# Waits and loads moved in four stages of a twelve-stage Perceiver kernel

## What is computed

```python
# layer 0 feed-forward ("fp4"): blocks of 16 are scaled, rounded to the FP4 grid, scaled back
xq, wq = fp4_quant_dequant(x), fp4_quant_dequant(w)
h = silu(xq_linear(x, w_gate)) * xq_linear(x, w_up); y = xq_linear(h, w_down)
# layer 1 cross-attention ("xattn1"): 16 heads of 16, biases bq, bk, bv, bo
attn = softmax(clip(q @ k.T * scale, -1e4, 1e4)); y = (attn @ v) @ Wo + bo
# layer 2 cross-attention ("xattn2"): 16 heads of 64, bias b_o
sim = softmax(q @ k.T * scale); y = (sim @ v) @ w_o + b_o
# layer 3 cross-attention ("xattn3"): one head of 256, both inputs layer-normed with gains and offsets
x1, x2 = layernorm(modality1, ln1_g, ln1_b), layernorm(modality2, ln2_g, ln2_b)
y = softmax((x1 @ Wq + bq) @ (x2 @ Wk + bk).T * E ** -0.5) @ (x2 @ Wv + bv) @ Wo + bo
```

## Time and profile before

| | us |
|---|---|
| median of three runs | 1784.45 |
| the three runs | 1783.11, 1784.45, 1786.04 |
| the profiled execution | 1781.79 |
| its span, first to last instruction | 1779.9 |
| TensorE busy | 1592.1 (89% of the span) |
| VectorE busy | 1069.7 (60%) |
| ScalarE busy | 849.0 (48%) |
| GpSimd busy | 771.7 (43%) |

### The profile page before, as it was taken

How to read it: one execution, slowest core, us unless ns; L and a number is a source line. 1 busy time by engine, 2 the same in 40 slices (tenths; PEclk the granted TensorE clock), 3 DMA queues, 4 the chain that set the end, 5 groups by cost and what they waited for, 6 DMA issues and landing times. The chain is left out here.

```text
span 1779.9 us, 37424 instructions
## 1 busy us (share of the span) xinstructions
PE 1592.1 (89%) x13583; PEld 1347.5 (76%) x13583; DVE 1069.7 (60%) x3001; ACT 849.0 (48%) x2446; POOL 771.7 (43%) x924
## 2 busy tenths in 40 slices
PE   7999999888886999987799999989978968859998
PEld 6898998756556999955799988965658934549997
DVE  5888887446855888845676677647971132363332
ACT  5666666355335888842566666641003312213332
POOL 7656656243338999833211111116743411212332
PEclk9999999999998999999999999999988987989999
DMA  8555454110023334302433333325028265771222
GB/s 274 168 174 161 151 174 153 64 63 2 1 83 98 137 130 139 119 19 71 171 122 102 125 104 103 126 79 182 1 54 263 29 179 163 249 243 35 37 38 30
DMA packets 127221, 205.30 MB, mean 115 GB/s; under 512 B 21034, under 2 KB 92362, under 8 KB 126530
## 3 DMA queue, kind: packets, MB, share of 16 engines
q1 hardware_dynamic: 119746, 193.61, 33.4%
q0 software_dynamic: 6720, 8.79, 3.2%
q10 hardware_dynamic: 576, 0.52, 0.1%
HBM read 162.54 MB, written 41.14 MB: 114 GB/s over the span
## 5 line engine op out<-in xcount | busy, mean ns | idle before, releaser
L879 DVE TENSOR_SCALAR xattn_oT<-banks,xattn_last 128x256 f32<-128x256 f32 x256 | 111.7, 478 | 90.8 <-PE banks L699 90.6
L785 ACT ACTIVATE xattn_probs<-banks,xattn_negmax 128x257 f32<-128x257 f32 x256 | 123.6, 483 | 67.5 <-DVE xattn_negmax L860 67.5
L1110 POOL TENSOR_SCALAR xattn_probs<-xattn_probs,xattn_rsum 128x257 f32<-128x257 f32 x128 | 119.6, 935 | 30.0 <-DVE xattn_rsum L1351 29.8
L790 ACT ACTIVATE xattn_probs<-xattn_probs,xattn_rsum 128x257 f32<-128x257 f32 x256 | 131.8, 515 | 1.4 <-DVE xattn_rsum L864 1.4
L860 DVE TENSOR_REDUCE xattn_negmax<-banks 128x1 f32<-128x257 f32 x256 | 106.4, 415 | 34.7 <-PE banks L672 33.3
L679 PE MATMUL banks<-ident,xattn_probs 128*128 128x128 f32 x512 | 104.2, 286 | 8.5 <-ACT xattn_probs L790 8.0
L796 ACT CAST xattn_probsT_hi<-banks 128x256 fp32r<-128x256 f32 x256 | 95.4, 372 | 32.7 <-PE banks L679 28.6
L869 DVE TENSOR_TENSOR xattn_probsT_lo<-banks,xattn_probsT_hi 128x256 fp32r<-128x256 f32 x256 | 104.9, 410 | 9.8 <-ACT xattn_probsT_hi L796 8.7
L617 POOL COPY ctx_stat<-xattn_mv 128x2 f32<-128x2 f32 x32 | 6.0, 187 | 238.2 <-DVE xattn_mv L893 238.2
L668 PE MATMUL banks<-xattn_ctxT,xattn_qk_hi 128*128 128x258 f32 x256 | 93.9, 367 | 0.5 <-POOL xattn_ctxN L585 0.3
L573 POOL TENSOR_SCALAR xattn_ctxT<-xattn_rawT 128x514 fp32r<-128x514 f32 x32 | 49.8, 1558 | 98.7 <-issue 94.4
(11 more groups left out here) (500 smaller groups left out, 5250.8 us busy)
## 6 DMA issues: line engine op xcount, KB each, us to landing
xattn_ctxT<-ctx_partsT SPq DMA_DIRECT2D x64, 516.0 KB, 4.0
xattn_ctxN<-ctx_partsN SPq DMA_DIRECT2D x64, 384.0 KB, 4.1
ctx_partsT<-xattn_ctxT SPq DMA_DIRECT2D x32, 516.0 KB, 2.8
moe_w<-in_L_ffn_W SPq DMA_DIRECT2D x16, 1024.0 KB, 13.6
ctx_partsN<-xattn_ctxN SPq DMA_DIRECT2D x32, 384.0 KB, 3.8
moecap_w_early<-in_L_ffn_w SPq DMA_DIRECT2D x10, 1024.0 KB, 9.2
xattn_N<-in_ctx_tiles SPq DMA_DIRECT2D x8, 776.0 KB
xattn_rawN<-in_ctx SPq DMA_DIRECT2D x32, 192.0 KB, 2.8
```

The source lines that it names most:

```text
L785: nc.scalar.activation(probs[:, n % RING, :], SB[n % 2][:, 0:KV], ACT.Exp, bias=negmax[:, n % RING:n % RING + 1], accum_out=psum[:, n % RI ...
L790: nc.scalar.mul(probs[:, n % RING, :], probs[:, n % RING, :], rsum[:, n % RING:n % RING + 1]).then_inc(norm_ready, 1)
L879: nc.vector.tensor_scalar(oT[k][:, heads, b, :], by_head(OB[:, k * 2 * P:(k + 1) * 2 * P]), last[:, k, j * PER_TILE + b:j * PER_TILE + b + ...
L1110: nc.gpsimd.tensor_scalar(probs[:, n % RING, :], probs[:, n % RING, :], rsum[:, n % RING:n % RING + 1], None, ALU.mult).then_inc(norm_read ...
```

## The change

Four edits, one in each stage.

1. xattn1: ScalarE's wait for wv and bv is moved from t = 0 into `values`.
2. xattn2: SP issues `raw_last` and raw rows 0 behind the parts of batch 0, and raw rows 1 behind the parts of batch 1. Raw rows 2 and 3 stay where they were.
3. fp4: ScalarE copies the turned chunk 0 out behind `x_parts(1)` and not behind `x_parts(3)`.
4. xattn3: `rstd` and `last_stat` become part of `ShortWeights` and are loaded at the end of SP's program for scan (22 DMAs on its semaphore and not 17). SP issues keys and rows of tiles 0 to 2 and keys 3, and then only keys 4 to 7. Rows 3 to 7 are issued by ScalarE, each behind `normalise(t - 3)`.

```diff
--- before.py
+++ after.py
@@ -357,6 +357,7 @@
     VALUES = (6, 7, 8, 9)
     PROJECT = {11: range(0, 3), 13: range(3, 6), 15: range(6, 8)}
     M_FILLS, M_START = 1 + GROUPS, 3
+    EARLY_ROWS = 2
     with ExitStack() as ctx:
         st = Stage(core, ctx, name)
         ln = Norm(st, shared=True, first=first)
@@ -476,6 +477,12 @@
                 sp.dma_start(ctxT[:, b].bitcast(F32), core.partsT[n]).then_inc(T_loaded[b], 16)
                 sp.dma_start(ctxN[:, b].bitcast(F32), core.partsN[n]).then_inc(N_loaded[b], 16)
 
+            def load_rows(n):
+                b = n % PER_TILE
+                if n >= PER_TILE:
+                    sp.wait_ge(stats_done, (n - PER_TILE + 1) * KCH)
+                sp.dma_start(raw[:, b], d["ctx_768"][n, 0:KCH * P, :].rearrange("(c p) f -> p c f", p=P)).then_inc(raw_loaded[b], 16)
+
             def keep_parts(n):
                 b = n % PER_TILE
                 sp.wait_ge(ctx_split, (n + 1) * PIECES)
@@ -497,6 +504,10 @@
             for n in range(PER_TILE):
                 if not first:
                     load_parts(n)
+                    if n == 0:
+                        sp.dma_start(raw_last[:, :], d["ctx_768"][:, KV - 1, :]).then_inc(raw_last_loaded, 16)
+                    if n < EARLY_ROWS:
+                        load_rows(n)
                 elif n < 2:
                     keep_parts(n)
                     load_raw(n + 2)
@@ -530,14 +541,7 @@
                 for b in range(PER_TILE):
                     sp.wait_ge(ctx_kept[b], TILES * 32)
             else:
-                def load_rows(n):
-                    b = n % PER_TILE
-                    if n >= PER_TILE:
-                        sp.wait_ge(stats_done, (n - PER_TILE + 1) * KCH)
-                    sp.dma_start(raw[:, b], d["ctx_768"][n, 0:KCH * P, :].rearrange("(c p) f -> p c f", p=P)).then_inc(raw_loaded[b], 16)
-
-                sp.dma_start(raw_last[:, :], d["ctx_768"][:, KV - 1, :]).then_inc(raw_last_loaded, 16)
-                for n in range(PER_TILE):
+                for n in range(EARLY_ROWS, PER_TILE):
                     load_rows(n)
                 for n in range(PER_TILE, BATCH):
                     sp.wait_ge(oT_ready, n // PER_TILE * UNITS + (n % PER_TILE + 1) * GROUPS - UNITS)
@@ -1296,6 +1300,7 @@
 
             def values(j, m):
                 act.wait_ge(m2_filled, j * 3 + m + 1)
+                act.wait_ge(wv_loaded, 64)
                 nc.scalar.activation(aT[:, m, :], M2[:, 0:P], ACT.Identity, bias=bv_s[:, m:m + 1]).then_inc(aT_ready, 1)
 
             fetch_table(core, ACT.Exp, unread)
@@ -1311,8 +1316,6 @@
             key_hi(0, 1)
             for t in range(ALL + UNITS):
                 j, s = divmod(t, UNITS)
-                if t == 0:
-                    act.wait_ge(wv_loaded, 64)
                 if 0 <= t - EXP < ALL:
                     exp(t - EXP)
                 if t < ALL and key_step(t):
@@ -2146,9 +2149,10 @@
                     x_parts(0)
                 act.wait_ge(turned, n + 1)
                 nc.scalar.copy(to, bank[n % WBANKS][0:rows, 0:len(sources) * P]).then_inc(turned_ready, 1)
-            for k in range(1, CHUNKS):
+            x_parts(1)
+            turned_x(0)
+            for k in range(2, CHUNKS):
                 x_parts(k)
-            turned_x(0)
             for s in range(TILES + 1):
                 if s < TILES:
                     silu(s)
@@ -3159,10 +3163,10 @@
 class ShortWeights:
 
 
-    PARTS = 17
-
-    def __init__(self, core, ctx):
-        self.core = core
+    PARTS = 22
+
+    def __init__(self, core, ctx, cn):
+        self.core, self.cn = core, cn
         self.CTX = CTX = core.dram["ctx_768"].shape[2]
         self.AUG, self.C2 = CTX + 2, CTX - P
         sb = lambda name, shape: ctx.enter_context(core.nc.sbuf_tensor(f"xattn3_{name}", shape, F32))
@@ -3173,6 +3177,7 @@
         self.sg1, self.sg2 = sb("sg1", [P, 2]), sb("sg2", [self.AUG - P, 2])
         self.gx, self.sx = sb("gx", [P, CD]), sb("sx", [P, CD])
         self.bo = sb("bo", [P, D])
+        self.rstd, self.last_stat = sb("rstd", [P, TILES, cn.KV]), sb("last_stat", [1, BATCH, 3])
         self.loaded = ctx.enter_context(core.nc.semaphore("xattn3_loaded"))
 
     def sp(self, sp):
@@ -3196,6 +3201,11 @@
             sp.dma_start(self.sg1[:, k:k + 1], column(name, 0, C1)).then_inc(self.loaded, 16)
             sp.dma_start(self.sg2[0:C2, k:k + 1], column(name, C1, CTX)).then_inc(self.loaded, 16)
 
+        sp.dma_start(self.last_stat[:, :, :], self.cn.ends.rearrange("(p b) k -> p b k", p=1)).then_inc(self.loaded, 16)
+        for b in range(PER_TILE):
+            sp.dma_start(self.rstd[b * SEQ:(b + 1) * SEQ, :, :],
+                         self.cn.rows[2, b:BATCH:PER_TILE, 0:self.cn.KV].partition_broadcast(SEQ)).then_inc(self.loaded, 16)
+
     def ready(self, eng):
         eng.wait_ge(self.loaded, 16 * self.PARTS)
 
@@ -3215,8 +3225,8 @@
         bq, bk, bv, bo, sg1, sg2, gx, sx = xw.bq, xw.bk, xw.bv, xw.bo, xw.sg1, xw.sg2, xw.gx, xw.sx
         T1, T2 = st.sb("T1", [P, RING, PER_TILE, KV]), st.sb("T2", [K2, RING, PER_TILE, KV])
         N = st.sb("N", [P, RING, PER_TILE, KCH, AUG])
-        N1, last_stat = st.sb("N1", [1, RING, PER_TILE, AUG]), st.sb("last_stat", [1, BATCH, 3])
-        rstd = st.sb("rstd", [P, TILES, KV])
+        N1 = st.sb("N1", [1, RING, PER_TILE, AUG])
+        rstd, last_stat = xw.rstd, xw.last_stat
         xT, qT = st.sb("xT", [P, CD, TOKENS]), st.sb("qT", [P, CD, TOKENS])
         qk1, qk2 = st.sb("qk1", [P, TOKENS]), st.sb("qk2", [K2, TOKENS])
         scaled = st.sb("scaled", [P, 2, KV])
@@ -3227,7 +3237,6 @@
         oT1, oT2 = st.sb("oT1", [P, 2, 2, P]), st.sb("oT2", [C2, 2, 2, P])
         aT = st.sb("aT", [P, 2, CD, 2 * P])
 
-        rstd_loaded, last_loaded = st.sem("rstd_loaded"), st.sem("last_loaded")
         T_loaded = [st.sem(f"T_loaded{z}") for z in range(RING)]
         N_loaded = [st.sem(f"N_loaded{z}") for z in range(RING)]
         ones_ready, moments_ready = st.sem("ones_ready"), st.sem("moments_ready")
@@ -3246,6 +3255,13 @@
         EXTRA = bank[6:8]
         block = ctx.enter_context(nc.Block())
 
+        def load_rows(eng, t):
+            z, sem = t % RING, N_loaded[t % RING]
+            if t >= RING:
+                eng.wait_ge(pv_done, t - RING + 1)
+            eng.dma_start(N[:, z].rearrange("p b c f -> p (b c f)"), d["ctx_tiles"][t]).then_inc(sem, 16)
+            eng.dma_start(N1[:, z].rearrange("p b f -> p (b f)"), d["ctx_ends"][t:t + 1, :]).then_inc(sem, 16)
+
         @block.sync
         def _(sp):
             def load_keys(t):
@@ -3256,22 +3272,12 @@
                 sp.dma_start(T2[0:C2, z].rearrange("p b k -> p (b k)"), of[C1:CTX, :]).then_inc(sem, 16)
                 sp.dma_start(T2[C2:K2, z], cn.rows[0:2, t * PER_TILE:(t + 1) * PER_TILE, 0:KV]).then_inc(sem, 16)
 
-            def load_rows(t):
-                z, sem = t % RING, N_loaded[t % RING]
-                if t >= RING:
-                    sp.wait_ge(pv_done, t - RING + 1)
-                sp.dma_start(N[:, z].rearrange("p b c f -> p (b c f)"), d["ctx_tiles"][t]).then_inc(sem, 16)
-                sp.dma_start(N1[:, z].rearrange("p b f -> p (b f)"), d["ctx_ends"][t:t + 1, :]).then_inc(sem, 16)
-
             load_keys(0)
-            sp.dma_start(last_stat[:, :, :], cn.ends.rearrange("(p b) k -> p b k", p=1)).then_inc(last_loaded, 16)
-            for b in range(PER_TILE):
-                sp.dma_start(rstd[b * SEQ:(b + 1) * SEQ, :, :],
-                             cn.rows[2, b:BATCH:PER_TILE, 0:KV].partition_broadcast(SEQ)).then_inc(rstd_loaded, 16)
-            load_rows(0)
-            for t in range(1, TILES):
+            for t in range(RING):
+                load_rows(sp, t)
+                load_keys(t + 1)
+            for t in range(RING + 1, TILES):
                 load_keys(t)
-                load_rows(t)
 
         @block.gpsimd
         def _(pool):
@@ -3285,10 +3291,9 @@
                 of = last_stat[:, t * PER_TILE:(t + 1) * PER_TILE, 0:2]
                 nc.gpsimd.tensor_copy(N1[:, t % RING, :, CTX:AUG], of).then_inc(moments_ready, 1)
 
-            pool.wait_ge(last_loaded, 16)
+            xw.ready(pool)
             for t in range(RING):
                 moments(t)
-            xw.ready(pool)
             ln.all_ready(pool)
             for t in range(TILES):
                 nc.gpsimd.tensor_tensor(core.x[:, t, :], core.x[:, t, :], bo[:, :], ALU.add).then_inc(bo_added, 1)
@@ -3484,6 +3489,8 @@
                     values((s - 5) // 2)
                 if 0 <= s - 2 < TILES:
                     normalise(s - 2)
+                    if s - 2 + RING < TILES:
+                        load_rows(act, s - 2 + RING)
 
         @block.vector
         def _(dve):
@@ -3538,8 +3545,6 @@
             ln.dve(dve)
             extra_columns()
             queries(0)
-            dve.wait_ge(rstd_loaded, 64)
-            dve.wait_ge(last_loaded, 16)
             for s in range(TILES + 5):
```

(2 more changed lines are left out.)

## The result

The changed kernel took 1763.18 us (median of 4 runs, 1759.81 to 1764.46) beside 1783.78 us for the kernel before: a ratio of 0.9881, 95% interval 0.9852 to 0.9910, 20.6 us less. The forecast was 1756.9, so 27.6 less. A second measurement on another chip gave 1764.61 against 1786.58, 0.9861 (0.9828 to 0.9895). The profiled execution went from 1781.79 to 1764.46 us, its span from 1779.9 to 1762.3.

A forecast was written before the change was run, and what follows sets the result against it. Each stage had its own bound: late loads in xattn1, xattn2 and xattn3, none to gain in fp4. 8.4 + 6.6 + 0 + 12.6 = 27.6 us gave 1754.2 profiled, 1756.9 as timed median; range 1751.2 to 1766.4.

The forecast's parts named there:

- rival B: xattn3: TensorE's clock falls in the new wait, or transfers come late; stage gains 7.6 us, total 1761.9; chance 0.18.
- xattn1, -8.4: xattn1: ScalarE's wait for bv at t = 0 goes and GpSimd, which sets the pace, shifts by 8.36 us.
- xattn2, -6.6: xattn2: without the wait for raw rows 0, exp(1) comes 5.2 us earlier and TensorE's kept clock gives 1.4 us.
- SyncE's 7.29 us at 0: xattn2: the issue of raw_last that held SP for 7.29 us was taken for a full queue and priced at 0.
- Rival C: xattn1 or xattn2: another load replaces the one removed; half of 8.4 + 6.6 goes, total 1764.4; chance 0.10.
- fp4, 0: fp4: the earlier copy gains 0.06 us at most, and VectorE covers the silu's 0.5 us delay; priced at 0.
- xattn3, -12.6: xattn3: earlier keys 4 give 15.3 us, less 2.7 us for a wait that turns up in their place.
- The 15.3 of full-clock steps: xattn3: from scores(4) on, steps at full clock bring scores(7) to 1484.8 and not 1500.12, 15.3 us sooner.
- The new wait: xattn3: late rows 5 delay GpSimd's bias adds, then VectorE's first add; TensorE stands at turn_out(4) for 2.7 us.
- That costs 2.7: xattn3: TensorE standing from 1486.2 to 1488.9 at turn_out(4) is priced at 2.7 us; bounds 0 and 4.0.
- ScalarE's issues at 0: xattn3: ten DMA issues on ScalarE, 0.45 us each or 0.9 us a step, fit its idle time; priced at 0.
- rival D: xattn3: an issue on ScalarE blocks as SP's did, 7.29 us, with exp behind it; slower, total 1815.4; chance 0.02.

The follow-up runs named there:

- xattn2 alone: Only raw_last and raw rows 0 and 1 issued earlier in xattn2, against the kernel before: 1776.18 us in one execution, the stage 344.75 us.

## Why the prediction was right, and where it wasn't

- **Total.** 1763.2 for a forecast of 1756.9: in the range, on the right side, 6.3 too low. It lies nearest to rival B (1761.9), to which 0.18 was given, and B's fall of the clock is what happened in xattn3. The range held the result because its low end was added up with B's 7.6 for that stage.
- **xattn1, -8.4.** Right in size and reason: 8.35 in the pair, with 8.36 at the very row named, and again with the edit alone. Over all profiles it is 7.2 (259.9 unedited, 252.7 edited), so the closeness of the pair is in part luck. That GpSimd sets the pace behind it held by the kernel without its adds.
- **xattn2, -6.6.** Right: 6.87 in the pair and 6.0 over all (351.5 and 345.5). Pricing SyncE's 7.29 us at 0 was right; the full queue behind it was not shown. Rival C, another load in place of the one removed, found no trace in either stage.
- **fp4, 0.** Right as far as can be seen: 31.05 and 31.08 us to the same turn. The stage as a whole comes in two lengths 1.9 us apart, with and without the edit, so the 0.33 says nothing.
- **xattn3, -12.6.** The mechanism was right and a term was missing from the sum. The 15.3 of full-clock steps measured 14.46, since the context products of step 6 waited 0.32 for rows 4 and scores(7) 0.80 for keys 7; the sum had neither. The new wait was sized well, 2.09 for 2.7: the last bias adds end 50.4 us into the stage, and 1487.1 less 1437.34, 49.8, was forecast. What failed is "That costs 2.7", which gave the wait as the whole price and put the clock behind it at nothing. I counted the gap's shortness, 2.7 us, against rival B; it was long enough, and the fall cost 4.4 us, twice the gap. B gave xattn3 7.6, and 7.94 was measured.
- **The base.** The rest of 24.33 at clock 1.00, from which the steps at full clock were laid, is the shortest of four executions with a mean of 29.3. Over these and the four profiles in which xattn3 is as in the change, the head gained 13.0 (60.9 to 47.9) and the rest lost 2.6 (29.3 to 31.9), which makes 10.4 for xattn3. With 7.2 and 6.0 that is 23.6, beside measured 20.6 and 22.0.
- **ScalarE's issues at 0.** Right: they took 0.31 to 0.54 us each, and rival D, an issue that blocks ScalarE, did not occur. The moved factors at 0 were right too, and were worth 0 as a gain.

## What to carry to other kernels

A load that stands behind another load's wait for a buffer is issued late by that wait; give the two different queues, and then look at what else was ordered behind the rows that now come late, here eight adds that had no reason to be there. Price a short hole on TensorE with the slow steps behind it: in one or two profiles each, filling it was worth twice the hole, and taking its cause away 2.5 times. Take a term from several profiles where a stage's length hangs on the clock, since one profile may be the best of them, as here.

## What the runs showed of the hardware

- An empty 2.1 us on TensorE, behind 0.8 us of waiting and between stretches at clock 1.00, was followed by 11 us at 0.54; the same time with matmuls in it by 23 us at 1.00. A single wait of 1.62, 1.88, 2.44, 2.77 or 2.91 us for keys 7 was followed by half speed at once; one of 1.70 (xattn2 alone) was not, nor were those of 0.20 to 1.05.
- The program's time goes roughly with the granted clock over the same instructions: of eleven runs of the kernel before, the one at 0.946 took 1796.9 us and the one at 0.964 1780.8. Of six runs of the changed kernel five took 1761.5 to 1766.4 us at 0.961 to 0.964, and one 1752.9 at 0.971. A stage that nobody touched came in a few separate lengths: lowrank 16.4 to 16.9 us at clock 1.00 and 17.6 to 18.2 at 0.90 or 0.91, attn3 49.9 in twelve profiles, at 1.00 or 0.97, and 51.22 in two, at 0.97.
